# LSTM recurrence on one core: K-tiles of every fourth row, 128-row weight loads, and a first step taken tile by tile

## The reference

```
xW = einsum('ntd,dk->tnk', x, Wx) + b
for t in 0..511:
    a = xW[t] + h @ Wh
    i, f, o = sigmoid(a[:, 0:512]), sigmoid(a[:, 512:1024]), sigmoid(a[:, 1024:1536])
    g = tanh(a[:, 1536:2048])
    c = f * c + i * g
    h = o * tanh(c)
    out[:, t] = x[:, t] + h
```

## Time and profile before

| what | value |
|---|---|
| median of 3 runs | 2592.07 us (2591.13 to 2594.83) |
| profiled execution, its own time | 2593.81 us |
| its span, first to last instruction | 2592.0 us |
| granted TensorE clock, mean | 0.998 |
| PE busy | 2526.8 us, 92166 matmuls |
| DVE busy | 1904.4 us |
| ACT busy | 1023.2 us |
| DMA | 76.17 MB, mean 29 GB/s |

### The profile page before, as it was taken

One profiled execution on the slowest core, in us unless ns is written; L12 is line 12 of the kernel. 1 busy time (PEld: TensorE's weight loads), 2 busy tenths in 40 slices (PEclk: granted clock), 3 DMA queues, 4 the chain that ended last, 5 costly groups with the idle time before them and its releaser, 6 DMA issues.

```text
span 2592.0 us, 201441 instructions
## 1 busy us (share of the span) xinstructions
PE 2526.8 (97%) x92166; PEld 2447.7 (94%) x92166; DVE 1904.4 (73%) x6324; ACT 1023.2 (39%) x3231; POOL 8.0 (0%) x20
## 2 busy tenths in 40 slices
PE   1999999999999999999999999999999999999998
PEld 1999999999999999999999999999999999999997
DVE  6677777777777777777777777777777777777775
ACT  4333343334334433433434433433343344343342
POOL 1000000000000000000000000000000000000000
PEclk9999999999999999999999999999999999999999
DMA  7010100101101101101101001011011011011000
GB/s 167 19 26 23 32 24 24 32 18 31 32 16 32 32 16 32 32 16 32 30 19 32 24 24 32 22 26 32 16 32 32 16 32 32 16 32 32 16 16 18
DMA packets 141594, 76.17 MB, mean 29 GB/s; under 512 B 8837, under 2 KB 140549, under 8 KB 140549
## 3 DMA queue, kind: packets, MB, share of 16 engines
q1 hardware_dynamic: 140096, 71.34, 11.0%
q0 software_dynamic: 768, 4.20, 0.7%
q10 hardware_dynamic: 708, 0.33, 0.1%
HBM read 42.27 MB, written 33.55 MB: 29 GB/s over the span
## 4 chain that ended last, share of the span: by engine, by line
PE 97%; DVE 1%; DMA 1%; issue 0%; ACTq 0%; ACT 0%; DVEq 0%
PE if_odd L221 26%; PE if_even L228 13%; PE og_even L228 13%; PE if_odd L228 13%; PE og_odd L228 13%; PE s1t_sum L221 6%; PE if_even L221 6%; PE og_even L221 6%; DMA bias_raw<-in_L_cond_b_dram 1%; DVE xw_lo L532 1%; DVE hw_lo L532 0%; DVE w_raw L561 0%; ACTq L389 0%; ACTq L386 0%; ACT tanh_c L354 0%
## 5 line engine op out<-in xcount | busy, mean ns | idle before, releaser
L492 DVE TENSOR_TENSOR i_g<-i_f,g_gate 128x128 f32<-128x128 f32 x512 | 149.3, 292 | 455.1 <-ACT g_gate L346 455.1
L221 PE MATMUL if_odd<-xw_hi,xT_hi 128*32 128x256 f16 x8192 | 402.5, 273 | 45.5 <-DVE xw_lo L532 37.5
L221 PE MATMUL if_odd<-xw_lo,xT_hi 128*32 128x256 f16 x8192 | 402.8, 273 | 0.2 <-issue 0.2
L221 PE MATMUL if_odd<-xw_hi,xT_lo 128*32 128x256 f16 x8192 | 402.6, 273 | 0.0
L221 PEld LDWEIGHTS if_odd<-xw_hi,xT_hi 128*32 128x32 f16 x8192 | 219.6, 97 | 51.8 <-DVE xw_lo L532 47.4
L354 ACT ACTIVATE tanh_c<-c_state 128x128 f32<-128x128 f32 x512 | 158.6, 310 | 192.6 <-DVE c_state L494 192.6
L221 PEld LDWEIGHTS if_odd<-xw_lo,xT_hi 128*32 128x32 f16 x8192 | 220.1, 97 | 5.1 <-issue 0.5
L221 PEld LDWEIGHTS if_odd<-xw_hi,xT_lo 128*32 128x32 f16 x8192 | 220.2, 97 | 4.7
L323 ACT ACTIVATE if_even<-if_odd 128x256 f32<-128x256 f32 x256 | 94.2, 368 | 259.8 <-PE if_odd L221 259.8
L490 DVE TENSOR_TENSOR f_c<-i_f,c_state 128x128 f32<-128x128 f32 x512 | 148.9, 291 | 64.3 <-ACT i_f L343 43.3
L343 ACT ACTIVATE i_f<-if_odd 128x256 f32<-128x256 f32 x256 | 98.4, 385 | 225.6 <-PE if_odd L228 225.6
(11 more groups left out here) (80 smaller groups left out, 5773.5 us busy)
## 6 DMA issues: line engine op xcount, KB each, us to landing
x_ring<-in_x_dram SPq DMA_DIRECT2D x256, 128.0 KB, 2.8
out_dram<-x_ring SPq DMA_DIRECT2D x252, 128.0 KB, 2.1
w_raw<-in_L_cond_Wx_dram POOLq DMA_DIRECT2D x8, 256.0 KB, 11.7
w_raw<-in_L_cond_Wx_dram SPq DMA_DIRECT2D x8, 256.0 KB, 17.8
w_raw<-in_L_cond_Wh_dram POOLq DMA_DIRECT2D x8, 256.0 KB, 25.0
w_raw<-in_L_cond_Wh_dram SPq DMA_DIRECT2D x8, 256.0 KB, 29.3
out_dram<-x_ring SPq DMA_DIRECT2D x8, 64.0 KB, 1.8
bias_raw<-in_L_cond_b_dram ACTq DMA_DIRECT2D x4, 64.0 KB, 15.5
```

The costliest lines, as they stand in the source:

```text
L221: mm = nc.tensor.matmul(bank[j * N:(j + 1) * N, 0:HALF], x_part[:, pair, n, k * N:(k + 1) * N], w_part[:, n, k, j, :], start=start and g = ...
L492: nc.vector.tensor_tensor(i_g[:, :], i_f[:, 0:P], g_gate[:, :], ALU.mult).then_inc(i_g_ready, 1)
```

## The change

K-tile k now holds rows 4p + k of the contraction, p being the partition. A weight tile is then one DMA of 128 rows of 8 KB, 32 KB apart, and SP issues all eight; POOL issues none. The transposes of h and x read every fourth column, so that the transposed tile has the same order.

```diff
-    w_v = [[w[j * P + k * N:j * P + (k + 1) * N, :] for j in range(J)] for w in (w_x, w_h) for k in range(J)]
+    w_v = [w.rearrange("(p k) c -> k p c", k=J)[k] for w in (w_x, w_h) for k in range(J)]
...
-                nc.vector.transpose(to[:, :], part[:, :]).then_inc(done, 1)
+                nc.vector.transpose(to[:, :].rearrange("p (k e) -> p k e", k=J),
+                                    part[:, :].rearrange("p (e k) -> p k e", k=J)).then_inc(done, 1)
...
-                src = x_now[:, :].rearrange("p (q s h f) -> p q s h f", q=2, s=2, h=2)
+                src = x_now[:, :].rearrange("p (q s e k) -> p q s k e", q=2, s=2, k=J)
```

```diff
             load_x(0, 0)
+            sp.wait_ge(bias_loaded, 16 * J)
             for n in range(2 * J):
-                for j in range(J // 2):
-                    sp.dma_start(w_raw[j * N:(j + 1) * N, n, :], w_v[n][j]).then_inc(w_loaded[n], 16)
+                sp.dma_start(w_raw[:, n, :], w_v[n]).then_inc(w_loaded[n], 16)
```

```diff
-            for n in range(2):
-                dve.wait_ge(w_loaded[n], 16 * (J // 2))
-                dve.wait_ge(w_loaded_pool[n], 16 * (J // 2))
-            difference(raw(0, 1), raw(0, 1), raw(0, 0), None)
-            split_x_lo(P_A11, 0, 0)
-            split_x_lo(P_S1, 0, 1)
...
+            for k in range(2):
+                dve.wait_ge(w_loaded[k], 16)
+                difference(raw(k, 1), raw(k, 1), raw(k, 0))
+                split_x_lo(P_A11, 0, 0, k)
+                split_x_lo(P_S1, 0, 1, k)
+            for k in range(2):
+                dve.wait_ge(w_loaded[2 + k], 16)
+                dve.wait_ge(xw_lo_ready[P_S1], k + 1)
+                difference(raw(k, 1), raw(2 + k, 1), raw(k, 1))
+                split_x_lo(P_A12, 2, 0, k)
+                split_x_lo(P_S4, 2, 1, k)
+                split_x_lo(P_S2, 0, 1, k)
             dve.wait_ge(bias_diff_ready, 2)
             take_s1t1(0)
...
+            for k in range(2):
+                difference(raw(k, 0), raw(k, 1), raw(k, 0))
+            for k in range(2):
+                difference(raw(2 + k, 0), raw(2 + k, 0), raw(k, 1))
+                split_x_lo(P_S3, 0, 0, k)
             fill_og_even(0, 0)
-            for k in range(J // 2):
-                split_h_lo(k)
+            for k in range(2):
+                split_x_lo(P_A22, 2, 0, k)
+            split_h_lo(0)
             fill_og_odd(0, 0)
-            for k in range(J // 2, J):
+            for k in range(1, J):
                 split_h_lo(k)
```

ACT's order follows, with `copy_even(1, 1)` behind the second tile of `Wh` in place of the fourth. The first recurrence takes each tile of `Wh` as it is split:

```diff
+            def recur_first():
+                pe.wait_ge(hT_lo_ready, 1)
+                for k in range(J):
+                    pe.wait_ge(hw_hi_ready, k + 1)
+                    for half, bank in enumerate((if_even[0], og_even)):
+                        recur_add(bank, half, hT_hi, hw_hi, k)
+                        recur_add(bank, half, hT_lo, hw_hi, k)
+                    pe.wait_ge(hw_lo_ready, k + 1)
+                    for half, bank in enumerate((if_even[0], og_even)):
+                        mm = recur_add(bank, half, hT_hi, hw_lo, k)
+                        if k == J - 1:
+                            mm.then_inc((if_gates_ready, og_gates_ready)[half], 1)
```

More of the change, by code:

```diff
@@ L103, in lstm_residual @@
         w_loaded = [sem(f"w_loaded{n}") for n in range(2 * J)]
-        w_loaded_pool = [sem(f"w_loaded_pool{n}") for n in range(2 * J)]
         bias_loaded = sem("bias_loaded")
@@ L204, in _ @@
             sp.wait_ge(out_stored, (CHUNKS + 1) * X_DMA)
[L206 to L210, removed]
         @block.tensor
@@ L231, in recur_add, with recur @@
                 return mm
-            def recur(t, s, weights=False):
+            def recur_first():
[10 more added lines that the diff above has]
+                            mm.then_inc((if_gates_ready, og_gates_ready)[half], 1)
+            def recur(t, s):
                 now = t + 1 if isinstance(t, int) else pe.snap(t + 1)
@@ L236, in recur @@
                 pe.wait_ge(hT_hi_ready, now)
-                if weights:
-                    pe.wait_ge(hw_lo_ready, J)
                 for half in range(2):
@@ L257, in middle @@
                 if weights:
-                    pe.wait_ge(xw_lo_ready[P_S1], 1)
+                    pe.wait_ge(xw_lo_ready[P_S1], 2)
                 else:
@@ L262, in middle @@
                 if weights:
-                    pe.wait_ge(xw_lo_ready[P_S2], 1)
+                    pe.wait_ge(xw_lo_ready[P_S2], 2)
                 pe.wait_ge(if_even_ready, q + 1)
@@ L266, in middle @@
                 if weights:
-                    pe.wait_ge(xw_lo_ready[P_A12], 1)
+                    pe.wait_ge(xw_lo_ready[P_A12], 2)
                 pe.wait_ge(late_ready, q + 1)
@@ L273, in close_even @@
                 if weights:
-                    pe.wait_ge(xw_lo_ready[P_S3], 1)
+                    pe.wait_ge(xw_lo_ready[P_S3], 2)
                 pe.wait_ge(og_even_ready, q + 1)
@@ L278, in close_even @@
                 if weights:
-                    pe.wait_ge(xw_lo_ready[P_S4], 1)
+                    pe.wait_ge(xw_lo_ready[P_S4], 2)
                 product(og_even, P_S4, p)
@@ L290, in step @@
                 q, p = c * (BODY // 2) + s // 2, s // 2 % 2
-                recur(t, s, weights=isinstance(t, int) and t == 0)
+                if isinstance(t, int) and t == 0:
+                    recur_first()
+                else:
+                    recur(t, s)
                 if s % 2 == 0:
@@ L305, in _ @@
             mm.then_inc(banks_open, 1)
-            pe.wait_ge(xw_lo_ready[P_A11], 1)
+            pe.wait_ge(xw_lo_ready[P_A11], 2)
             open_pair(0, 0)
@@ L370, in split_hi, with split_x_hi @@
                 return nc.scalar.activation(dst, src, ACT.Copy, scale=WSCALE)
[L372 to L377, removed]
+            def split_x_hi(n, k0, gates, k):
+                split_hi(w_raw[:, k0 + k, gates * HALF * J:(gates + 1) * HALF * J]
+                         .rearrange("p (g j f) -> p g j f", g=2, j=J),
+                         xw_hi[:, n, k, :, :].rearrange("p j (g f) -> p g j f", g=2)).then_inc(xw_hi_ready[n], 1)
             def split_h_hi(k):
@@ L402, in _ @@
             seed(1)
-            for n in range(2):
[L404 to L413, removed]
-            copy_even(0, 0)
[L415 to L420, removed]
+            for k in range(2):
+                act.wait_ge(w_loaded[k], 16)
+                split_x_hi(P_A11, 0, 0, k)
+                act.wait_ge(w_diff_ready, k + 1)
+                split_x_hi(P_S1, 0, 1, k)
+            for k in range(2):
+                act.wait_ge(w_loaded[2 + k], 16)
+                split_x_hi(P_A12, 2, 0, k)
+                split_x_hi(P_S4, 2, 1, k)
+                act.wait_ge(w_diff_ready, 2 + k + 1)
+                split_x_hi(P_S2, 0, 1, k)
+            copy_even(0, 0)
+            for k in range(2):
+                act.wait_ge(w_diff_ready, 4 + k + 1)
+                split_x_hi(P_S3, 0, 0, k)
+            for k in range(2):
+                act.wait_ge(w_diff_ready, 6 + k + 1)
+                split_x_hi(P_A22, 2, 0, k)
             for k in range(J):
-                act.wait_ge(w_loaded[J + k], 16 * (J // 2))
-                act.wait_ge(w_loaded_pool[J + k], 16 * (J // 2))
+                act.wait_ge(w_loaded[J + k], 16)
                 split_h_hi(k)
-            copy_even(1, 1)
+                if k == 1:
+                    copy_even(1, 1)
             act.wait_ge(s2_done, 1)
@@ L533, in split_lo, with split_x_lo @@
                                                       op0=ALU.mult, op1=ALU.subtract)
[L535 to L542, removed]
+            def split_x_lo(n, k0, gates, k):
+                dve.wait_ge(xw_hi_ready[n], k + 1)
+                src = w_raw[:, k0 + k, :].rearrange("p (g j f) -> p g j f", g=GATES, j=J)
+                hi = xw_hi[:, n, k, :, :].rearrange("p j (g f) -> p g j f", g=2)
+                lo = xw_lo[:, n, k, :, :].rearrange("p j (g f) -> p g j f", g=2)
+                for g in range(2):
+                    v = split_lo(src[:, 2 * gates + g, :, :], hi[:, g, :, :], lo[:, g, :, :])
                 v.then_inc(xw_lo_ready[n], 1)
@@ L552, in split_h_lo, with raw, difference @@
                 v.then_inc(hw_lo_ready, 1)
[L554 to L560, removed]
+            def raw(k, gates):
+                return w_raw[:, k, gates * HALF * J:(gates + 1) * HALF * J]
+            def difference(to, a, b):
                 nc.vector.tensor_tensor(to, a, b, ALU.subtract).then_inc(w_diff_ready, 1)
@@ L583, in _ @@
                                     op0=ALU.mult).then_inc(bias_diff_ready, 1)
-            for n in range(2):
-                dve.wait_ge(w_loaded[n], 16 * (J // 2))
-                dve.wait_ge(w_loaded_pool[n], 16 * (J // 2))
-            difference(raw(0, 1), raw(0, 1), raw(0, 0), None)
-            split_x_lo(P_A11, 0, 0)
-            split_x_lo(P_S1, 0, 1)
[L590 to L599, removed]
+            for k in range(2):
[3 more added lines that the diff above has]
```

(21 more changed lines are left out.)

4 lines of the change are left out of this document (2 added, 2 removed).

## The result

The changed kernel took 2576.95 us (median of 4 runs, 2575.01 to 2577.66); the kernel before took 2591.84 us beside it. The ratio is 0.9937, with a 95% interval of 0.9925 to 0.9949. 2575 was forecast, in a range of 2568 to 2592. The profiled execution took 2577.3 us and its span is 2575.5, so the span became 16.5 us shorter.

What follows compares the result with a forecast made beforehand. PE was taken to bound the loop, with DVE's weight block, released late by the bias load, in front; 14.5 + 2.5 = 17.0 us off the 2592.0 span gave 2575, range 2568 to 2592 (own range 2571 to 2579).

Steps and rivals of the forecast that it cites:

- Part 1: Loads at the kernel's start: small loads land near 6.0 us, weight tile 0 at 12.4, further tiles 4.2 us apart.
- a single queue: Weight loads: one queue carries 200 GB/s or less, or the bias is slow; 2578 to 2585, chance 0.08.
- Part 2: DVE's work on h0, x and the bias before the weights: DVE is ready at 12.6 us, just after tile 0.
- part 5: Strided transposes of h and x: h costs nothing more, x up to 248 ns more, hidden by DVE's idle time.
- Part 3: DVE's weight work in the prologue: 37.2 us from 12.8, last split of Wh ends at 50.8, 14.5 us earlier.
- ACT's order: ACT's splits in the prologue: split_h_hi(2) ends near 46, just before DVE asks; a miss costs under 1 us.
- Part 4: From the last split to the second recurrence: 3.9 us where it took 6.4, a gain of 2.5.
- the forecast's other case: First recurrence: if PE's bursts on each tile keep the clock high, 1.3 us more are gained.
- The surcharge d: Extra time of each strided h transpose, two per step in the loop's chain; taken as zero, 0.124 us at half rate.
- rival A: The loop pays for the stride, 2d - 0.06 us a step: 2611 or 2671, by reference figures 2630 to 2730; chance 0.18.
- The room of 0.06 us: Slack in each loop step: gates, cell and transposes need 4.85 us, PE 4.91.

Runs made afterwards that it cites:

- e6: The changed kernel with each weight tile loaded as four pieces of 32 rows, all from SP: 2578.68 us.
- e3: The changed kernel without SP's wait for the bias before the weight loads: 2589.25 us.
- e5: The changed kernel with DVE and ACT starting a tile of Wx only when both tiles of its pair have landed: 2577.01 us.
- e7: The changed kernel with h_hi and h_lo in every second fp16 slot, so h transposes read with a 16-byte step, not 8: 2659.71 us.
- e9: The changed kernel with five matmuls of zeros behind the high parts of each of the last three Wh tiles in the first recurrence: 2573.78 us.
- e4: The changed kernel with the first recurrence in one piece again, after all four Wh tiles are split: 2580.44 us.
- e1: The kernel before with the new row order alone, transposes reading every fourth column, weight loads as before: 2593.46 us.
- e2: The kernel before with the load order alone: bias ahead of h0, SP and POOL waiting for the bias before the weight pieces: 2586.60 us.
- e8: The changed kernel with part of DVE's weight work and the bias difference on GpSimd, ACT's hw_hi of tile 0 earlier, h0 before the bias: 2581.87 us.
- e11: The changed kernel with h0 issued ahead of the bias on ACT's queue and the bias difference made by GpSimd: 2575.22 us.
- e10: The changed kernel with the edits of e9 and e11 together: 2571.14 us.

## Why the prediction was right, point by point

**The frame held.** The loop is PE's, the prologue is DVE's, and a change of order moves the start of DVE's block. Predicted 17.0 us off the span, measured 16.5. Part of this closeness is luck. The sum was 14.5 (the last split) and 2.5 (the first recurrence); they measured 14.4 and 1.5, and the remaining 0.6 us lie behind the second recurrence, where the sum has no term. The median, 2576.95, is 2 us over the forecast and within its own range.

**Part 1, loads.** The small loads land at 7.1 to 7.2, not at 6.0. The tiles' 4.2 us were wrong by far: at 426 GB/s a tile takes 2.5. The term was taken from the rate of 32-row loads, and no row of before could show another. The forecast feared a single queue; e6 shows that the queue has nothing to do with it. The error cost the sum no more than its 0.8 us of tile waits, because DVE needs 3.6 to 4.9 us a tile itself, near the 4.2 that the forecast gave the load.

**Part 2, DVE ahead of the weights.** 12.6 was forecast and 14.26 measured: 1.2 us for `h0` landing at 7.19, and about 0.5 for the x work (8.21 to 13.60, 5.4 us in place of 4.8), whose surcharge part 5 had left to the tile waits to absorb. There were none left to do so.

**Part 3, the block.** 37.2 us of work and 0.8 of waits were forecast, 36.7 measured (14.26 to 50.94). The end, 50.8, came out at 50.94 by luck: a start 1.5 us later than the 12.8 that the forecast counted from was made up by the 0.8 us of waits that did not come and by 0.5 us less work. ACT's order, named as the closest, held.

**Part 4, first recurrence.** 3.9 us forecast, 4.9 measured. This term was mis-sized. In the profiled execution the clock did not rise after 2.5 us but stayed at the lower level until 56. Where the clock was high (e3, e5, e7, e9) the stretch is 2.7 to 2.8 us (51.37 to 54.03 in e9), which is the forecast's other case. e4 prices the tile-by-tile order at 3.4 us by the medians and at 2.0 with the low clock in both profiles, against the 2.5 of the forecast.

**Part 5, the stride.** Right for h (312 to 315 ns), right for x within its bound of 248 (217), and right that the loop hides it (e1). That h would be free was a choice of the nearer end and had no row behind it; e1 and e7 came after. The surcharge d was 3 ns at most, so rival A, with its 2611 to 2730, did not come. The room of 0.06 us was tested by e7, which shows that there is one and not that it is just 0.06.

**Attribution.** What no sum could give is how the edits share the 15 us. The load order alone has 6 of them (e2). The first recurrence has 2.0 to 3.4 (e4). The rest is DVE's not having to wait for a pair of tiles: 5 to 6 us by subtraction of the medians, 8.4 in the end of the last split in the profiles. The two figures differ because the stretch behind the last split varies with the clock, by 2.2 us in these profiles and in e2 by more (7.8 us there), so the shares are rough. For this part 128-row loads alone would have done (e5), and per-tile waits alone nearly (e6). SP's wait is the condition for all of it: without it 12 us are lost. The row order by itself costs and brings nothing clear of the noise; what it permits is the faster load, 1.2 to 1.7 us here.

## What to carry to other kernels

When one engine's block sets a stretch, look at what releases its first instruction, and then at the first instruction in its queue, not at the one that seems to matter: here a 64 KB load ahead in the queue was worth 12 us of waiting. A transfer that is small and needed first should be landed before the bulk is issued. Before a rate is put into a sum, ask of what shape of transfer it was measured.

## What the runs showed of the hardware

- Rate by rows in one DMA: 8 KB rows moved at 219 GB/s in 32-row loads (256 KB, e6) and at 426 GB/s in 128-row loads (1 MB), on the same queue.
- DVE's 32x32 transpose: a source step of 8 bytes costs 3 ns at most (312 to 315 ns for 128 fp16 columns, 312 before), a step of 16 bytes 0.84 ns a column for fp16 (312 to 420) and 0.85 for fp32 (436 to 653).
- GpSimd beside DVE (e8): while elementwise work of 12 us ran on GpSimd, DVE's operations with two inputs took 2.2 to 2.5 times as long on the mean, one of them 4.40 us in place of 1.2. DVE's transposes, with one input, took no longer beside 1.6 us of GpSimd work (e11).
- TensorE's clock: after bursts that filled 1.5 of 5 us it was at 1.2 GHz for the 92 matmuls that followed in the changed kernel's two profiles, and at 2.4 GHz in those of e3, e5 and e7; with 15 matmuls of zeros in the gaps (busy 4.0 of 5 us) it was at 2.4 GHz in both profiles (e9, e10), and these kernels were the fastest, with the gap at the loop's end gone as well.
- The granted clock can read 1.00 where 100 matmuls take 5.00 us (e1, 66 to 71 us); at 2.4 GHz they take 27.3 ns each.
- PE's gap on leaving the loop (2.4 to 3.1 us) is there in the profiles of eleven kernels of this case and absent in two (e9, e10), which alone have 15 matmuls more in PE's program; its cause stays open.
